# Issuing the context loads of a gated cross-attention kernel from ScalarE's queue instead of SyncE's

## The chip, the cores and the metric

The kernel runs on one core of a Trainium2 chip. A core has five engines with a queue of instructions each: TensorE (PE, matmuls), VectorE (DVE), ScalarE (ACT), GpSimd (POOL) and SyncE (SP). SyncE does no arithmetic; it waits for semaphores and issues transfers (DMAs). ScalarE and GpSimd can issue transfers too. The metric is the device time of one execution in microseconds.

## The reference

The kernel computes one gated cross-attention block and one gated feed-forward block for 32 batches. The queries come from `x` (32 x 100 x 256), keys and values from a context `ctx` (32 x 1444 x 256); there are 16 heads of 16.

```python
h = layernorm(x)
q, k, v = h @ Wq.T + bq, ctx @ Wk.T + bk, ctx @ Wv.T + bv
p = softmax(where(mask, clip(q @ k.T / 4, -50, 50), -50))       # per head
delta = clip(residual_scale, 0, 0.3) * ((p @ v) @ Wo.T + bo)
x = x + tanh(g_xattn) * (norm(delta) * ln_gamma + ln_beta)
x = x + tanh(g_ffn) * ffn(layernorm(x))     # quantized, silu(a) * b, hidden 704
```

## The kernel before, in words

**Tiles and steps.** The 1444 context rows of a batch are cut into NT = 12 tiles of 121 rows (the last has 113), and the tiles into three pieces of four, u = 0, 1, 2. A batch is 12 steps on every engine, n = 0 to 11, one for each tile of scores. Each engine has its own hand-written program; semaphores order them.

**The way of a piece.** `load_c(b, u)` copies a piece of the transposed context from HBM into one of two buffers `c_in` (128 partitions, 2 x 484 floats each). VectorE splits it into a high and a low part, `c_hi` (line 763) and `c_lo` (line 769); the latter raises `split_done` under the names `lo0`, `lo1`, `lo2`. After `c_lo` the buffer `c_in` is free. TensorE computes keys and values from the parts (lines 1293 and 1307), ScalarE and VectorE write the keys' parts `k_hi` and `k_lo`, ScalarE the values `v_sb`. `stack_k(b, u)` on SyncE then copies the keys with 12 transfers of about 121 KB from buffer to buffer into `k_st`, in the layout that the score matmuls read (line 331). `k_st` has two slots for three pieces, so `stack_k` first waits until the scores that read the slot are done (line 328). The scores of steps 0, 4 and 8 wait for the landing of the stack of piece 0, 1 and 2. POOL issues 12 smaller transfers that stack the next batch's queries (`q_st`, line 492) at its step 8.

**When.** Context work runs ahead. In batch b, TensorE computes from step 4 on the keys and values of pieces 0 and 1 of batch b + 1, and in steps 0 to 3 those of piece 2 of b itself. So the stack of piece 0 of batch b + 1 starts after the scores of step 7 of batch b (they free its slot), and must have landed by step 0 of batch b + 1.

**A step.** On TensorE: four score matmuls, half a context item, some other work, sometimes the attention matmuls (`pv`, line 1272, 128 at once in steps 1, 5 and 9), four score matmuls again, the other half of the item. On ScalarE: an item of the context work (`k_hi` or `v_sb`), an exponential of the first scores (line 572), other work, an exponential of the second scores. There are two score banks in turn, so each score matmul waits for the exponential before the last. The feed-forward work is done for groups of 128 rows; 25 such groups end in the 32 batches, so 7 batches (0, 4, 9, 13, 18, 22 and 27) complete none. The batches behind these, and batch 0, have shorter steps in their second half.

**The order of SyncE's queue in a batch** is: stack of piece 1; x of batch b + 2; residual rows; wait for `lo0` of b + 1; load of piece 2 of b + 1; store of a finished group; stack of piece 2; wait for `lo1`; load of piece 0 of b + 2; stack of piece 0 of b + 1; wait for `lo2`; load of piece 1 of b + 2.

The first pieces, before the loop over batches, are loaded from SyncE too. The line numbers are those of the kernel before.

Of the kernel before, what the change touches and what calls it, by code (L numbers as in the profile page):

```python
# [37 lines left out]
def whole(n, base=0):  # L38
    return Batch(base + n, (base + n) // 2, n % 2, base)


def flamingo_block(nc, x, ctxT, maskT, g_xattn, g_ffn, wqT, bq, wkT, bk, wvT, bv, woT, bo,
# [22 lines left out]
    NB, S, H = x.shape  # L65
    T = ctxT.shape[2]
    F = w1T.shape[1]
    P = 128
# [13 lines left out]
    CW = TPC * TT  # L82
    CL = [sum(TL[TPC * u:TPC * (u + 1)]) for u in range(NCH)]
# [24 lines left out]
    with es:  # L108
        def sb(name, shape, dt=f32):
            return es.enter_context(nc.sbuf_tensor(name, shape, dt))  # L110
# [4 lines left out]
        def sem(name):  # L115
            return es.enter_context(nc.semaphore(name))
# [39 lines left out]
        c_in = [sb(f"c_in{i}", [P, KT, CW]) for i in range(2)]  # L156
# [48 lines left out]
        c_loaded = [sem(f"c_loaded{i}") for i in range(2)]  # L205
# [11 lines left out]
        split_done, k_lo_done = sem("split_done"), sem("k_lo_done")  # L217
# [6 lines left out]
        SPLIT = Steps(*(f"{p}{u}" for u in range(NCH) for p in ("hi", "lo")))  # L224
# [31 lines left out]
        def c_slot(b, u):  # L256
            g = b.plus(u)
            before = 3 * b.pair + (3 * b.par + u) // 2
            return g.par, before


        def e_slot(b, n):
            return (NT * b.par + n) % NE

        def full_group(b):

            g = S * (b.row + 1) // P - 1
            if b.row < 0 or g < S * b.row // P:
                return None
            return whole(g, NG if b.base else 0)  # L270
# [38 lines left out]
        def _(sp):  # L309
            def load_x(b):  # L310
                sp.dma_start(x_in[b.par][:, :], x[bass.ds(b.row, 1), :, :].rearrange("o s h -> (o s) h")
                             ).then_inc(x_loaded[b.par], 16)

            def load_c(b, u):
                slot, _n = c_slot(b, u)
                src = ctxT[bass.ds(b.row, 1), :, u * CW:u * CW + CL[u]]
                sp.dma_start(c_in[slot][:, :, 0:CL[u]], src.rearrange("o (k p) t -> p (o k) t", p=P)
                             ).then_inc(c_loaded[slot], 16)

            def stack_k(b, u):  # L320
                slot, _n = c_slot(b, u)
                sp.wait_ge(k_lo_done, KE.after(b, f"{u}{KT - 1}"))
                if not (isinstance(b.n, int) and b.n == 0 and u < NKS):

                    ob, ou = (b, u - NKS) if u >= NKS else (b.plus(-1), u - NKS + NCH)
                    if b.base:
                        sp.sem_inc(waited_sp, 1)
                    sp.wait_ge(sc_ready, SCORE.after(ob, STEPS * TPC * (ou + 1) - 1))
                for j in range(NQ):
                    for part, src in enumerate((k_hi, k_hi, k_lo)):  # L330
                        sp.dma_start(k_st[st_slot(b, u)][QR * part:QR * (part + 1), :, j, 0:CL[u]].bitcast(f32),  # L331
                                     src[slot][QR * j:QR * (j + 1), :, 0:CL[u]].bitcast(f32)
                                     ).then_inc(k_stacked[u], 16)

            def store(g):
                sp.wait_ge(result_done, g.n + 1)
                sp.dma_start(out_rows[P * g.row:P * (g.row + 1), :], y_out[:, :]).then_inc(stored, 16)

            def load_res(g):
                if g.row >= 2:  # L340
                    sp.wait_ge(dve_post, D_V.after(g.plus(-2), "x1"))
                elif g.base:
                    sp.wait_ge(dve_post, D_V.after(whole(NG - 1), "x1"))
                sp.dma_start(x_res[g.par][:, :], x_rows[P * g.row:P * (g.row + 1), :]).then_inc(res_loaded[g.par], 16)
# [21 lines left out]
            def batch(b, own, nxt, nxt2):  # L366
                if own:
                    stack_k(b, 1)
                if nxt2:
                    sp.wait_ge(dve_x, X_V.after(b, "xn"))  # L370
                    load_x(b.plus(2))
                if full_group(b):
                    load_res(full_group(b))
                if nxt:
                    sp.wait_ge(split_done, SPLIT.after(b.plus(1), "lo0"))
                    load_c(b.plus(1), 2)
                if full_group(b.plus(-2)):
                    store(full_group(b.plus(-2)))
                stack_k(b, 2)
                if nxt2:  # L380
                    sp.wait_ge(split_done, SPLIT.after(b.plus(1), "lo1"))
                    load_c(b.plus(2), 0)
                if nxt:
                    stack_k(b.plus(1), 0)
                if nxt2:
                    sp.wait_ge(split_done, SPLIT.after(b.plus(1), "lo2"))
                    load_c(b.plus(2), 1)

            def passes(base):
                if base:  # L390
# [149 lines left out]
        def _(act):  # L540
# [21 lines left out]
            def magnitudes(i):  # L562

                act.wait_ge(s_w, 16 * 6)
                nc.scalar.activation(unused[i], weights[i], ACT.Abs, accum_out=wabs[:, i:i + 1]).then_inc(s_seta, 1)

            def exps(b, n, k):
                q = n * STEPS + k
                act.wait_ge(sc_ready, SCORE.after(b, q))
                if k == 0 and not (isinstance(b.n, int) and b.n == 0 and n < NE):  # L570
                    act.wait_ge(pv_done, TILE.after(b, n) - NE)
                nc.scalar.activation(e_sb[e_slot(b, n)][0:TL[n], k * SW:(k + 1) * SW].rearrange("p (o c) -> p o c", o=2),  # L572
                                     sc[q % NSC][0:TL[n], :, 0:2 * PW],
                                     ACT.Exp, scale=HD ** -0.5).then_inc(exp_done, 1)
# [28 lines left out]
            def ctx_item(b, w):  # L603
                u, r = divmod(w, 4)
                if r < 2:
                    k_head(b, u, r)
                else:
                    v_out(b, u, r - 2)
# [21 lines left out]
            def h_turned(b):  # L630
                act.wait_ge(pe_post, D_T.after(b, "hT"))
                nc.scalar.activation(hT[:, :, :], mb16[:, 0:FT * P].rearrange("p (k s) -> p k s", k=FT), ACT.Copy
                                     ).then_inc(act_post, 1)
# [10 lines left out]
                act.wait_ge(pe_post, D_T.after(b, f"u{i}"))  # L644
                nc.scalar.activation(us[:, cols], mb[:, 0:FH], ACT.Copy, scale=tiny[:, 5:6]).then_inc(act_post, 1)

            def batch(b, own, nxt):
                c, gd, ge = b.plus(1), full_group(b.plus(-1)), full_group(b.plus(-2))
                for n in range(NT):
                    if n < ITEM + 1 and own:  # L650
                        ctx_item(b, n - (ITEM + 1) + NT)
                    if n >= ITEM + 1 and nxt:
                        ctx_item(c, n - (ITEM + 1))
                    exps(b, n, 0)
                    if ge and n == 1:
                        h_turned(ge)
                    if nxt and n == 4:
                        x_turned(c)
                    if nxt and n == 5:
                        x_query(c)  # L660
                    if gd and n == 7:
                        x2_turned(gd)
                    if gd and n in (9, 10):
                        ffn_up(gd, n - 9)
                    if gd and n in (8, 9):
                        ffn_gate(gd, n - 8)
                    exps(b, n, 1)

            def passes(base):
                act.wait_ge(s_setv, SETV["bqm11"])  # L670
                x_turned(whole(0, base))
                x_query(whole(0, base))
                for w in range(NT - (ITEM + 1)):
                    ctx_item(whole(0, base), w)
                    if w >= 3 and not base:
                        for i in range(2 * w - 6, min(2 * w - 4, 6)):
                            magnitudes(i)
                act.wait_ge(s_setv, SETV["bv"])
                act.wait_ge(s_setp, SETP["rest"])
                act.wait_ge(s_seta, SETA["abs5"])  # L680
                for n in range(NB - 1):
                    batch(whole(n, base), True, True)
                e = whole(NB - 1, base)
                batch(e, True, False)
                last = full_group(e)
                h_turned(last.plus(-1))
                x2_turned(last)
                for i in range(2):
                    ffn_gate(last, i, sc[0][:, i, :])
                    ffn_up(last, i, sc[1][:, i, :])  # L690
                h_turned(last)

            passes(0)
            again(act, passes)

# [823 lines left out]
```

## Time and profile before

| | |
|---|---|
| median of 3 runs | 1332.48 us (1331.07 to 1334.24) |
| the profiled execution | 1329.38 us, span 1327.6 us |
| TensorE busy | 1282.6 us |
| VectorE busy | 1069.2 us |
| ScalarE busy | 947.9 us |
| GpSimd busy | 394.4 us |
| granted TensorE clock, mean | 0.987 |

The span is the time from the first to the last instruction that the profiler saw; what lies around it makes the rest of the execution's time. Busy times of the engines overlap each other. The matmuls are pipelined and their ends are modelled, so TensorE can show as busy while it stalls briefly. Issuing a transfer does not count as busy time of an engine; such instructions are listed under the engine's name with a q (SPq, ACTq).

### The profile page before, as it was taken

What the parts mean: (1) busy time and instruction counts of PE and PEld (TensorE: products, weight loads), DVE (VectorE), ACT (ScalarE), POOL (GpSimd) and SP (SyncE); (2) the same over time, 40 slices, a digit from 0 to 9 for tenths busy, and PEclk for the clock granted to TensorE, in tenths of its full rate; (3) what the DMA queues carried; (4) which work ended last, traced back from release to release, by engine and by line L of the source; (5) the groups of instructions that cost most, each with busy time, mean ns of one, the idle gap of its engine ahead of it and who ended that gap; (6) DMA issues with size and microseconds to landing.
All of it is one profiled execution on the core that took longest, in us unless ns stands there. A gap on an engine that the chain in (4) does not pass through costs nothing.

```text
span 1327.6 us, 47302 instructions
## 1 busy us (share of the span) xinstructions
PE 1282.6 (97%) x19802; PEld 1177.7 (89%) x19802; DVE 1069.2 (81%) x2085; ACT 947.9 (71%) x1561; POOL 394.4 (30%) x695
## 2 busy tenths in 40 slices
PE   5999999999999999999999999999999999999983
PEld 4988998999999999999999999999999999999972
DVE  5777888779888789886888886888778889778864
ACT  4766777677777767776767776777777877777761
POOL 4322333222333231322331323331233331133310
PEclk9999999999999999999999999999999999999986
DMA  8867777677777777777676768766777776777630
GB/s 238 204 161 180 168 171 183 168 173 182 170 170 184 174 175 174 169 170 197 171 171 168 178 160 203 174 168 160 175 188 176 180 170 163 179 182 175 149 78 11
DMA packets 146187, 225.38 MB, mean 170 GB/s; under 512 B 29674, under 2 KB 139310, under 8 KB 145966
## 3 DMA queue, kind: packets, MB, share of 16 engines
q1 hardware_dynamic: 132312, 202.06, 62.5%
q0 software_dynamic: 12288, 19.69, 6.4%
q8 instruction: 158, 2.59, 0.9%
q10 hardware_dynamic: 1366, 0.53, 0.2%
q14 instruction: 63, 0.52, 0.1%
HBM read 57.27 MB, written 3.28 MB: 46 GB/s over the span
## 4 chain that ended last, share of the span: by engine, by line
PE 89%; SPq 4%; DVE 3%; DMA 2%; issue 1%; ACT 1%; POOL 0%; DVEq 0%; POOLq 0%; ACTq 0%
PE sc L1252 23%; PE pvb L1272 20%; PE cb L1307 19%; PE cb L1293 18%; SPq L331 4%; PE mb L1367 2%; PE mb L1335 2%; PE mb L1345 2%; DMA k_st<-k_lo 1%; PE mb L1382 1%; DVE zt L880 1%; PE mb L1374 1%; PE mb L1328 0%; DMA c_in<-in_ctxT 0%; DVE k_lo L793 0%
## 5 line engine op out<-in xcount | busy, mean ns | idle before, releaser
L572 ACT ACTIVATE e_sb<-sc 121x800 f32<-121x800 f32 (+1 forms) x768 | 644.7, 844 | 187.2 <-PE sc L1252 176.5
L1252 PE MATMUL sc<-q_st,k_st 96*121 96x200 f32 (+1 forms) x3072 | 469.4, 275 | 8.3 <-DMA k_st<-k_lo 5.2
L1252 PEld LDWEIGHTS sc<-q_st,k_st 96*121 96x121 f32 (+1 forms) x3072 | 411.1, 185 | 40.0 <-issue 9.0
L802 DVE TENSOR_SCALAR e_sb<-e_sb,hi_b 121x1600 f32<-121x1600 f32 (+1 forms) x384 | 404.2, 1056 | 12.3 <-ACT e_sb L572 12.1
L1272 PE MATMUL pvb<-e_sb,v_sb 121*32 121x100 f32 x12288 | 286.5, 251 | 0.0
L1272 PEld LDWEIGHTS pvb<-e_sb,v_sb 121*32 121x32 f32 x12288 | 265.2, 110 | 23.5 <-issue 20.4
L793 DVE SCALAR_TENSOR_TENSOR k_lo<-cb,bk_c,k_hi 128x484 fp32r<-128x484 f32 (+1 forms) x192 | 134.5, 701 | 132.8 <-ACT k_hi L584 132.5
L492 POOL DMA_DIRECT2D q_st<-bd_hi x256 | 157.5, 619 | 269.2 <-DVE bd_lo L848 263.8
L1307 PE MATMUL cb<-wv_hi,c_hi 128*121 128x256 f32 (+1 forms) x768 | 221.7, 289 | 2.4 <-DVE k_lo L793 1.3
L1307 PE MATMUL cb<-wv_hi,c_lo 128*121 128x256 f32 (+1 forms) x768 | 215.6, 281 | 0.0
L1307 PE MATMUL cb<-wv_lo,c_hi 128*121 128x256 f32 (+1 forms) x768 | 215.5, 281 | 0.0
L1293 PE MATMUL cb<-c_hi,wk_hi 128*128 128x484 f32 (+1 forms) x384 | 153.7, 400 | 0.0
L1293 PE MATMUL cb<-c_hi,wk_lo 128*128 128x484 f32 (+1 forms) x384 | 146.3, 381 | 0.0
L1293 PE MATMUL cb<-c_lo,wk_hi 128*128 128x484 f32 (+1 forms) x384 | 146.2, 381 | 0.0
L1307 PEld LDWEIGHTS cb<-wv_hi,c_hi 128*121 128x121 f32 (+1 forms) x768 | 141.2, 184 | 4.4 <-DVE k_lo L793 4.4
L1307 PEld LDWEIGHTS cb<-wv_hi,c_lo 128*121 128x121 f32 (+1 forms) x768 | 140.3, 183 | 0.0
L1307 PEld LDWEIGHTS cb<-wv_lo,c_hi 128*121 128x121 f32 (+1 forms) x768 | 139.6, 182 | 0.0
L584 ACT ACTIVATE k_hi<-cb,bk_c 128x484 fp32r<-128x484 f32 (+1 forms) x192 | 127.0, 661 | 1.3 <-PE cb L1293 1.3
L769 DVE TENSOR_TENSOR c_lo<-c_in,c_hi 128x968 fp32r<-128x968 f32 (+1 forms) x96 | 118.7, 1237 | 0.0
L463 POOL TENSOR_SCALAR d_ve<-dmv,scal 128x1 f32<-128x1 f32 x25 | 10.9, 438 | 344.2 <-DVE dmv L907 344.2
L593 ACT ACTIVATE v_sb<-cb 121x512 f32<-121x512 f32 x160 | 96.1, 600 | 5.3 <-PE cb L1307 5.3
L492 POOL DMA_DIRECT2D q_st<-bd_lo x128 | 88.2, 689 | 0.1
(160 smaller groups left out, 1351.1 us busy)
## 6 DMA issues: line engine op xcount, KB each, us to landing
k_st<-k_hi SPq DMA_DIRECT2D x512, 121.0 KB, 3.0
c_in<-in_ctxT SPq DMA_DIRECT2D x64, 484.0 KB, 3.9
k_st<-k_lo SPq DMA_DIRECT2D x256, 121.0 KB, 3.2
k_st<-k_hi SPq DMA_DIRECT2D x256, 119.0 KB, 3.3
c_in<-in_ctxT SPq DMA_DIRECT2D x32, 476.0 KB, 3.8
k_st<-k_lo SPq DMA_DIRECT2D x128, 119.0 KB, 3.0
q_st<-bd_hi POOLq DMA_DIRECT2D x256, 50.0 KB, 3.3
q_st<-bd_lo POOLq DMA_DIRECT2D x128, 50.0 KB, 3.2
```

Of the source, the lines that this page charges most:

```text
L331: sp.dma_start(k_st[st_slot(b, u)][QR * part:QR * (part + 1), :, j, 0:CL[u]].bitcast(f32), src[slot][QR * j:QR * (j + 1), :, 0:CL[u]].bitc ...
L492: nc.gpsimd.dma_start(q_st[b.par][QR * part:QR * (part + 1), :, j, :].bitcast(f32), src[QR * j:QR * (j + 1), :, :, :].rearrange("p k a s - ...
L572: nc.scalar.activation(e_sb[e_slot(b, n)][0:TL[n], k * SW:(k + 1) * SW].rearrange("p (o c) -> p o c", o=2), sc[q % NSC][0:TL[n], :, 0:2 * PW],
L584: nc.scalar.activation(k_hi[slot][:, o, 0:CL[u]], cb[o][:, 0:CL[u]], ACT.Identity, bias=bk_c[:, o:o + 1]).then_inc(k_hi_done, 1)
L593: nc.scalar.activation(v_sb[0:TL[n], n:n + 2, :, 0:4:3, :].rearrange("p n q a d -> p (n q) a d"), cb[i][0:TL[n], :].rearrange("p (q a d) - ...
L769: V.tensor_tensor(c_lo[slot][:, :, 0:w], c_in[slot][:, :, 0:w], c_hi[slot][:, :, 0:w].bitcast(f32), ALU.subtract).then_inc(split_done, 1)
L793: V.scalar_tensor_tensor(k_lo[slot][:, o, 0:w], cb[o][:, 0:w], bk_c[:, o:o + 1], k_hi[slot][:, o, 0:w].bitcast(f32), ALU.add, ALU.subtract ...
L802: V.tensor_scalar(e, e, E_LO, hi_b[b.par][0:TL[n], n:n + 1], ALU.max, ALU.min).then_inc(clip_done, 1)
L1252: last = T_.matmul(sc[q % NSC][0:TL[n], e // 2, (e % 2) * PW:(e % 2 + 1) * PW], k_st[st_slot(b, n // TPC)][:, pr // NQ, pr % NQ, t0:t0 + T ...
L1272: last = T_.matmul(pvb[QR * j:QR * (j + 1), col:col + S], v_sb[0:TL[n], n, pr, 2 * a:2 * a + 2, :].rearrange("p x d -> p (x d)"), e[0:TL[n ...
L1293: last = T_.matmul(cb[o][:, 0:w], wt[:, k, o * P:(o + 1) * P], ct[slot][:, k, 0:w], start=i == 0, stop=i == 5)
L1307: last = T_.matmul(cb[i][0:TL[n], half * H:(half + 1) * H], ct[slot][:, k, t0:t0 + TL[n]], wt[:, k, :], start=(k == 0 and a == 0), stop=(k ...
```

## The change

The three loads of a batch and the waits ahead of them leave SyncE's queue. ScalarE gets a `load_c` of its own and issues the same three transfers, behind the same waits, at the end of step 4 (piece 2 of batch b + 1), step 7 (piece 0 of b + 2) and step 11 (piece 1 of b + 2), each behind the second exponential of that step. The loads before the loop over batches stay on SyncE.

```diff
             def batch(b, own, nxt, nxt2):
...
-                if nxt:
-                    sp.wait_ge(split_done, SPLIT.after(b.plus(1), "lo0"))
-                    load_c(b.plus(1), 2)
                 if full_group(b.plus(-2)):
                     store(full_group(b.plus(-2)))
                 stack_k(b, 2)
-                if nxt2:
-                    sp.wait_ge(split_done, SPLIT.after(b.plus(1), "lo1"))
-                    load_c(b.plus(2), 0)
                 if nxt:
                     stack_k(b.plus(1), 0)
-                if nxt2:
-                    sp.wait_ge(split_done, SPLIT.after(b.plus(1), "lo2"))
-                    load_c(b.plus(2), 1)
...
+            def load_c(b, u):
+                slot, _n = c_slot(b, u)
+                src = ctxT[bass.ds(b.row, 1), :, u * CW:u * CW + CL[u]]
+                act.dma_start(c_in[slot][:, :, 0:CL[u]], src.rearrange("o (k p) t -> p (o k) t", p=P)
+                              ).then_inc(c_loaded[slot], 16)
...
                     exps(b, n, 1)
+                    if nxt and n == 4:
+                        act.wait_ge(split_done, SPLIT.after(c, "lo0"))
+                        load_c(c, 2)
+                    if nxt and nxt2 and n == 7:
+                        act.wait_ge(split_done, SPLIT.after(c, "lo1"))
+                        load_c(b.plus(2), 0)
+                    if nxt and nxt2 and n == 11:
+                        act.wait_ge(split_done, SPLIT.after(c, "lo2"))
+                        load_c(b.plus(2), 1)
```

## Rows read from the trace of the kernel before

**Rows 1.** The page: busy time, share of the span, instructions

```profile
PE 1282.6 (97%) x19802; PEld 1177.7 (89%) x19802; DVE 1069.2 (81%) x2085; ACT 947.9 (71%) x1561; POOL 394.4 (30%) x695
```

**Rows 2.** Waits, all engines: us in total, times, longest

```profile
PEld sc L1252 <- DMA k_st<-k_lo: 7.3, 10, 1.6
```

**Rows 3.** Waits of SyncE's queue: us in total, times, longest

```profile
SPq L317 <- DVE c_lo L769: 110.2, 30, 6.1
```

**Rows 4.** Timeline of SyncE in batch 9: start, duration (us), what

```profile
408.93 0.59 SPq L317 DMA_DIRECT2D c_in<-in_ctxT  x1
412.72 1.23 SPq L331 DMA_DIRECT2D k_st<-k_hi  x2
...
421.34 1.61 SPq L331 DMA_DIRECT2D k_st<-k_lo  x1
423.00 0.59 SPq L317 DMA_DIRECT2D c_in<-in_ctxT  x1
```

**Rows 5.** Timeline of TensorE, score matmuls of batches 9 to 11

```profile
411.98 0.65 PE L1252 MATMUL sc<-q_st,k_st 96*121 96x200 f32 x4
...
415.69 0.58 PE L1252 MATMUL sc<-q_st,k_st 96*121 96x200 f32 x4
...
426.32 0.58 PE L1252 MATMUL sc<-q_st,k_st 96*121 96x200 f32 x4
...
428.48 0.57 PE L1252 MATMUL sc<-q_st,k_st 96*121 96x200 f32 x4
...
464.23 0.67 PE L1252 MATMUL sc<-q_st,k_st 96*121 96x200 f32 x4
```

**Rows 6.** Transfers into k_st, window 422 to 423 (the issue from 421.34)

```profile
DMA to landing us min/median/max: 3.8/3.8/3.8
```

**Rows 7.** Timeline of SyncE in batch 10, first and last issue of the stack

```profile
451.80 1.22 SPq L331 DMA_DIRECT2D k_st<-k_hi  x2
...
461.83 0.60 SPq L331 DMA_DIRECT2D k_st<-k_lo  x1
```

**Rows 8.** Transfers into k_st, window 462 to 463 (the issue from 461.83)

```profile
DMA to landing us min/median/max: 2.4/2.4/2.4
```

**Rows 9.** Timeline of SyncE: first issue of the first and last of 31 stacks

```profile
54.76 1.23 SPq L331 DMA_DIRECT2D k_st<-k_hi  x2
...
1243.27 1.23 SPq L331 DMA_DIRECT2D k_st<-k_hi  x2
```

**Rows 10.** Stretch 413 to 426: busy by engine, granted clock, DMA share, GB/s

```profile
413.00:426.00 13.00, 13.00 (x205) 11.58 (x205) 9.23 (x18) 10.49 (x19) 7.79 (x14) 1.00 0.83 197
```

**Rows 11.** Timeline of SyncE: first issue, first and last of 28 piece-1 stacks

```profile
146.52 0.59 SPq L331 DMA_DIRECT2D k_st<-k_hi  x1
...
1216.16 1.23 SPq L331 DMA_DIRECT2D k_st<-k_hi  x2
```

**Rows 12.** Issues of line 317: duration ns minimum/median/maximum, first and last start

```profile
L317 SPq DMA_DIRECT2D c_in<-in_ctxT x96: 372/586/1616, 1.7 to 1229.8; - x96
```

**Rows 13.** Timeline of VectorE in batch 9, c_lo of piece 1

```profile
406.89 1.16 DVE L769 TENSOR_TENSOR c_lo<-c_in,c_hi 128x968 fp32r<-128x968 f32 x1
```

**Rows 14.** Timeline of ScalarE: exponentials of steps 7, 8 and the next 0

```profile
412.66 0.84 ACT L572 ACTIVATE e_sb<-sc 121x800 f32<-121x800 f32 x1
...
413.88 0.83 ACT L572 ACTIVATE e_sb<-sc 121x800 f32<-121x800 f32 x1
...
427.02 0.84 ACT L572 ACTIVATE e_sb<-sc 121x800 f32<-121x800 f32 x1
```

**Rows 15.** Timeline of ScalarE's queue at the start

```profile
1.70 0.51 ACTq L544 DMA_DIRECT2D bk_c<-in_bk  x1
```

**Rows 16.** The page, DMA issues: count, KB each, median us to landing

```profile
c_in<-in_ctxT SPq DMA_DIRECT2D x64, 484.0 KB, 3.9
```

**Rows 17.** The page, DMA queues: packets, MB, share of 16 engines' span

```profile
q1 hardware_dynamic: 132312, 202.06, 62.5%
q0 software_dynamic: 12288, 19.69, 6.4%
```

More of the change, by code:

```diff
@@ L645, in ffn_up, with batch @@
                 nc.scalar.activation(us[:, cols], mb[:, 0:FH], ACT.Copy, scale=tiny[:, 5:6]).then_inc(act_post, 1)
-            def batch(b, own, nxt):
+            def batch(b, own, nxt, nxt2=False):
                 c, gd, ge = b.plus(1), full_group(b.plus(-1)), full_group(b.plus(-2))
@@ L680, in passes @@
                 act.wait_ge(s_seta, SETA["abs5"])
-                for n in range(NB - 1):
-                    batch(whole(n, base), True, True)
+                for n in range(NB - 2):
+                    batch(whole(n, base), True, True, True)
+                batch(whole(NB - 2, base), True, True)
                 e = whole(NB - 1, base)
```

## The prediction, made before the changed kernel was timed

> **What bounds the kernel now.** I read the page's busy shares first. TensorE is busy 1282.6 us, 97% of the span [rows 1]. So a transfer can cost or give time only where it makes TensorE wait, and the first question is for which transfers it waits. In the view of waits the largest one in the steady part is the stacked keys', 7.3 us in 10 pieces on the weight load's side [rows 2]. No wait for a context piece stands there. On SyncE's queue 110.2 us go to the waits for c_lo ahead of a load, which the change takes off that queue [rows 3]. That is idle time of a queue, and it matters only if what is queued behind comes late.
>
> Next I put the three stacks of a batch beside their deadlines. Piece 0 of the next batch is the tight one. In batch 9 its first issue starts at 412.72 us [rows 4], freed by the second scores of step 7 (411.98, 0.65 long) [rows 5]. Its last issue starts at 421.34 and lands 3.8 us later, at 425.2 [rows 4, 6]. TensorE wants it at 426.32 [rows 5]: latency 12.5 us, room 13.6 us. Batch 10 has no row group to finish, so its steps are shorter: start 451.80, last issue 461.83, landing 2.4 us on, at 464.2, where the scores start at once, at 464.23 [rows 5, 7, 8]. There the room is 12.4 us and nothing is spare. I took the latency of all 31 such stacks (the first issued at 54.76, the last at 1243.27 [rows 9]): 11.5 to 14.7 us, mean 12.8; 12.4 in the 8 short batches, 13.0 in the 23 long ones.
>
> Why is this stack slow? Its 12 issues go out two in 1.23 us when nothing holds them, so all in some 7.7 us; here they take 10.2, the last alone 1.61 [rows 4]. POOL issues the query stack in the same stretch (its step 8), and the DMA share there is 0.83 [rows 10]. The stack of piece 1, without POOL's transfers beside it, has a mean latency of 11.1 us over the 28 of batches 3 to 30 (the first from 146.52, the last from 1216.16 [rows 11]).
>
> **The change, part by part.**
>
> *SyncE loses three issues and three waits.* One issue is 0.37 to 1.62 us, median 0.59 [rows 12]. Piece 2's load stands just ahead of the stack of piece 2. That stack can start up to one issue earlier, but TensorE is not seen waiting for it in the steady part: worth nothing. Piece 1's load (423.00) follows the tight stack, and the next stack must wait for the last scores of the batch anyway: nothing in issue time. The tight stack itself waits for scores 7 and not for the load ahead of it, issued 3.8 us before [rows 4]: nothing.
>
> *ScalarE gains three waits and three issues.* The waits are met: c_lo of piece 1 ends at 408.05 [rows 13], and step 7 ends on ScalarE at 413.50 [rows 14]; the other two stand likewise. The bounds of an issue are 0.37 and 1.62 us, SyncE's fastest and slowest of the same transfer [rows 12]. I take 0.6: its median, and close to the 0.51 that an issue on ScalarE takes at the start, at 1.70, beside the first of SyncE's loads at 1.7 [rows 12, 15]. Queued behind step 7's issue are a copy to v_sb and the exponential that ends at 413.88 + 0.83 = 414.71 [rows 14]; TensorE's scores of step 9 need its bank at 415.69 [rows 5]: cover 1.0 us. Behind step 11's are a copy and the exponential that ends at 427.86 [rows 14], which the scores of step 1 need at 428.48 [rows 5]: cover 0.6 us. Behind step 4's come the attention matmuls of step 5, when ScalarE idles. So the issues cost 0 at my value. At 1.62 us the two exposed places cost 0.6 + 1.0 us a batch, 48 us over 30 batches, the far bound.
> The Trainium skill (Perfetto Trace Analysis, "DMA Instruction — HWDGE (DVE, Sync)") says that a sequencer must lock the descriptor generator for itself and that the profiled duration holds the wait for that lock. By it a ScalarE issue could take its own time plus one of SyncE's, an estimate of 1.2 us, and cost 0.6 us a batch at the tighter place; the two side by side at the start do not bear that out.
>
> *The loads move in time and to another queue.* This decides. Piece 2's goes from just ahead of its batch's stack of piece 2 into that stack. Piece 1's goes from 423.00 to just before the exponential at 427.02 [rows 4, 14], into the stack of the next piece 1, which has the room: four steps. Piece 0's was issued at 408.93 and landed about 3.9 us later [rows 4, 16], just when the tight stack starts. It goes to 413.5, 0.8 us *after* that start, into the stretch where POOL's transfers run too.
>
> What do a load's 484 KB [rows 16] cost there? Queue 1 spends 62.5% of 16 engines' span on 202.06 MB, 4.1 us per MB, so a load (0.496 MB) is 2.0 us of all engines. The query stack is 6.4% of the span over 32 batches, 2.7 us each [rows 17]. Lower bound of the delay: 0 (a gain is the second rival). The share of 0.83 over 13 us leaves 2.2 us idle, which could hold all of it; and the mean latency of 11.1 us of piece 1 is had with a load ahead of it in the same queue. Upper bound: all 2.0 us plus one issue of 0.6, so 2.6 us. Nearest row: POOL's 2.7 us. The stack takes 11.1 us without it and 12.8 with it: 1.7 of 2.7, two thirds. Two thirds of 2.0 is 1.3; I take off 0.3, because piece 1's load no longer follows the stack's last pieces closely. Delay 1.0 us.
> The Trainium skill (DMA: Bandwidth & Descriptors, "Queues, rings and completion order") has each DMA engine serve its queues in turn, packet by packet. Where SyncE's queue kept the load ahead of the stack or behind it, a second queue mixes it in; that speaks for a full delay while all three queues have work. With 2.0 us the same sum below would give 42 us.
>
> **Sum.** The delay counts only beyond the room. The 8 short batches have none, so each pays nearly all: 6.6 us (batch 0 has 0.9 us spare). Of the 22 long ones with a moved load, six have latencies of 13.5 or more and pay nearly all, 5.9 us; the other 16 have 0.6 to 1.4 us spare and pay 1.6 between them. Together 14.1 us. On the profiled execution's 1329.4 us (span 1327.6 and 1.8 around it) that is 1343.5. The median of the runs is 3.1 us above that execution, so 1346.6: I say 1347. The same adding for other delays: 0.5 gives 6 us, 1.5 gives 28, 2.6 gives 60.
>
> **Rivals.**
> - *The load is absorbed.* For it: idle DMA time of 2.2 us in the stretch, and piece 1's example. By the skill's section "Issuing engines are not separate DMA queues" (same page) the same 16 engines carry the same bytes and only issue time is saved. Time: delay under 0.25 us, 0 to 2.5 us, 1332 to 1335.
> - *Faster: SyncE's lighter queue ends the waits for stacked keys.* The tight stack's last pieces would no longer share the engines with piece 1's load, issued 0.05 us after them. If that shortens the landing by more than the moved load costs (those of two last pieces took 3.8 and 2.4 us [rows 6, 8]), the steady waits vanish; those are 3.5 us by my sum, and at most the 7.3 us of rows 2. Time: 1326 to 1329. Against it: the load is back after the stack's landing, and one as large is put into its middle.
> - *ScalarE pays.* Its issues take over 1.2 us because SyncE's issues are stuck behind full queues. It decides from 0.6 us on at step 0. Time: +10 to +48 us, 1342 to 1380.
>
> **How the numbers follow.** Stacked keys late: 0.60. Absorbed: 0.20. Faster: 0.14. ScalarE pays: 0.06. Least that can be told from no change is 0.2%, 2.7 us. Some of the first case's small delays fall within it, some of the absorbed one's outside: faster 0.14, same 0.21, slower 0.65. The likeliest case alone spans 1337 to 1375 (delay 0.5 to 2.0). For 8 in 10, I go from 1331 (nearly all of the faster case left out) to 1369 (delay up to 1.8).
>
> **What would show it.** In the changed kernel: piece 0's load on ScalarE's queue starts 0.7 to 1.0 us after the stack's first issue; more of that stack's issues take over 1 us; its latency goes from 12.8 to near 13.8; the waits for k_st by TensorE rise from 7 to about 20 us, nearly all at step 0 of a batch, most in the short ones. The durations of ScalarE's issues stay below 1 us, and waits for e_sb do not grow. I am wrong if the latency stays at 12.8 (absorbed) or falls (faster), or if the new idle time of TensorE is before scores and released by ScalarE.

## The result, and the profile after

The changed kernel takes 1350.89 us, the median of 4 runs (1348.23 to 1356.21). The kernel before, run beside it, takes 1333.35 us (4 runs, 1331.07 to 1334.24). The ratio is 1.0138 [1.0115, 1.0162]: slower by 17.5 us. The prediction was 1347.0, range 1331 to 1369. The profiled execution took 1348.23 us, with a span of 1346.3 us (before: 1327.6). The mean granted clock is 0.986, as good as the 0.987 of before, so the time is not a matter of the clock.

The page of the changed kernel: busy times, then two queues of part 3 (packets, MB, share of 16 engines' span), then the shares of the chain that ended last, then the transfers (KB each, median us from issue to landing).

```profile
PE 1290.9 (96%) x19802; PEld 1182.0 (88%) x19802; DVE 1069.6 (79%) x2085; ACT 950.2 (71%) x1561; POOL 392.2 (29%) x695
...
q1 hardware_dynamic: 107560, 157.21, 49.7%
q10 hardware_dynamic: 26118, 45.38, 13.5%
...
PE 75%; SPq 12%; DMA 6%; DVE 3%; issue 2%; ACT 1%; POOL 0%; DVEq 0%; POOLq 0%
...
c_in<-in_ctxT ACTq DMA_DIRECT2D x60, 484.0 KB, 4.6
```

No engine has more work than in [rows 1], to within 1%. Queue 1 (SyncE's) carries 44.85 MB less than in [rows 17], and queue 10 (ScalarE's), which had 0.53 MB before, carries just that much more. The bytes did not change, only their queue and their moment. The chain now runs for 12% through SyncE's issues and for 6% through transfers, where before it had 4% and 2%:

```profile
PE 89%; SPq 4%; DVE 3%; DMA 2%; issue 1%; ACT 1%; POOL 0%; DVEq 0%; POOLq 0%; ACTq 0%
```

The waits of the changed kernel (total us, times, longest):

```profile
PEld pvb L1279 <- issue: 25.0, 68, 1.6
PEld sc L1259 <- DMA k_st<-k_lo: 16.4, 21, 2.0
PE sc L1259 <- DMA k_st<-k_lo: 11.8, 16, 1.8
PE pvb L1279 <- issue: 3.6, 5, 1.4
...
PE sc L1259 <- ACT e_sb L569: 1.9, 4, 0.6
```

The wait for stacked keys grew by 9.1 us from the 7.3 of [rows 2]. A second wait grew too, "issue" at the attention matmuls, where nothing that the profile shows is waited for. Here is the same view of the kernel before:

```profile
PEld pvb L1272 <- issue: 20.4, 64, 0.6
```

Its total rose by 4.6 us: 3.1 us of that stand at step 1, in several batches, and 1.6 us at step 9, where one batch (28) has the longest, 1.6.

Now the tight stack that is issued in batch 9, which [rows 4] show before. SyncE's timeline in the changed kernel (start, duration, what):

```profile
419.04 1.23 SPq L331 DMA_DIRECT2D k_st<-k_hi  x2
...
422.23 1.37 SPq L331 DMA_DIRECT2D k_st<-k_lo  x1
423.64 2.06 SPq L331 DMA_DIRECT2D k_st<-k_hi  x2
...
427.83 0.96 SPq L331 DMA_DIRECT2D k_st<-k_lo  x1
432.18 1.23 SPq L331 DMA_DIRECT2D k_st<-k_hi  x2
```

ScalarE's timeline in the same moment:

```profile
419.00 0.84 ACT L569 ACTIVATE e_sb<-sc 121x800 f32<-121x800 f32 x1
419.00 0.37 ACTq L561 DMA_DIRECT2D c_in<-in_ctxT  x1
419.74 0.59 ACT L590 ACTIVATE v_sb<-cb 121x512 f32<-121x512 f32 x1
```

The load is issued at 419.00, 0.04 us before the stack's first issue. It takes 0.37 us, while ScalarE's exponential runs, and the copy behind is not held up. These are the landings of the stack's transfers issued from 419.04 and, below, of those issued from 427.83:

```profile
DMA to landing us min/median/max: 5.1/5.1/5.1
...
DMA to landing us min/median/max: 5.3/5.3/5.3
```

Before, the last one took 3.8 us [rows 6], and the first, in the view of transfers from 412.8 to 413:

```profile
DMA to landing us min/median/max: 2.4/2.4/2.4
```

So the stack of batch 9 lands at 427.83 + 5.3 = 433.1, 14.1 us after its start (12.5 before), and TensorE waits for it at step 0 (timeline of TensorE, changed kernel; in brackets the idle time before):

```profile
431.54 0.56 PE L1259 MATMUL sc<-q_st,k_st 96*113 96x200 f32 x4
...
433.19 0.67 PE L1259 MATMUL sc<-q_st,k_st 96*121 96x200 f32 x4 [0.37 <-DMA k_st<-k_lo]
```

**Where the 18.7 us of span went.** I read the start of each group of score matmuls in both traces and added up, over the batches, by how much each interval between two neighbouring groups grew.

| place | growth, us |
|---|---|
| last scores of step 11 to first scores of step 0 | 8.0 |
| step 0 itself | 1.2 |
| step 1, and the interval behind it | 4.6 + 0.8 |
| from the second scores of step 10 to the first of step 11 | 0.4 |
| step 9 itself (1.7 in batch 28, 0.8 in batch 31) | 2.5 |
| until the first scores of batch 1 | 1.6 |
| sum | 19.1 |

What lies behind the last scores is 0.4 us shorter. The stall for keys explains half (9.2 us, which fits the 9.1 in the waits). As the prediction said, most of it falls on the short batches: 5.7 of the 8.0 us. The 4.6 at step 1 equals the 4.6 by which "issue" rose only by chance, since 1.6 of the latter stand at step 9. The idle time before a matmul shows less than the delay, because the ends of matmuls are modelled. These growths are differences of two single executions. How much two profiles of one kernel differ is told at the end of the experiments.

### The profile page after: what moved, and what is told of

It reads as the page before. It is cut to its first block, busy times and chain, and to the rows that moved or that the text cites. A ratio compares the mean times of both kernels' runs of the same rounds, so it can differ in the third digit from the quotient of the medians.

```text
span 1346.3 us, 47302 instructions
## 1 busy us (share of the span) xinstructions
PE 1290.9 (96%) x19802; PEld 1182.0 (88%) x19802; DVE 1069.6 (79%) x2085; ACT 950.2 (71%) x1561; POOL 392.2 (29%) x695
## 4 chain that ended last, share of the span: by engine, by line
PE 75%; SPq 12%; DMA 6%; DVE 3%; issue 2%; ACT 1%; POOL 0%; DVEq 0%; POOLq 0%
PE sc L1259 19%; PE pvb L1279 17%; PE cb L1300 15%; PE cb L1314 15%; SPq L331 12%; DMA k_st<-k_lo 5%; PE mb L1342 2%; PE mb L1352 2%; PE mb L1374 2%; PE mb L1389 1%; PE mb L1381 1%; DVE zt L887 1%; DMA c_in<-in_ctxT 0%; PE mb L1335 0%; DVE k_lo L800 0%
## 5 line engine op out<-in xcount | busy, mean ns | idle before, releaser
L1259 PEld LDWEIGHTS sc<-q_st,k_st 96*121 96x121 f32 (+1 forms) x3072 | 410.8, 185 | 48.7 <-DMA k_st<-k_lo 16.4
L809 DVE TENSOR_SCALAR e_sb<-e_sb,hi_b 121x1600 f32<-121x1600 f32 (+1 forms) x384 | 405.5, 1058 | 14.6 <-ACT e_sb L569 14.3
L483 POOL DMA_DIRECT2D q_st<-bd_lo x128 | 85.0, 664 | 0.1
```

The lines of the kernel that those rows point to most:

```text
L483: nc.gpsimd.dma_start(q_st[b.par][QR * part:QR * (part + 1), :, j, :].bitcast(f32), src[QR * j:QR * (j + 1), :, :, :].rearrange("p k a s - ...
L809: V.tensor_scalar(e, e, E_LO, hi_b[b.par][0:TL[n], n:n + 1], ALU.max, ALU.min).then_inc(clip_done, 1)
L1259: last = T_.matmul(sc[q % NSC][0:TL[n], e // 2, (e % 2) * PW:(e % 2 + 1) * PW], k_st[st_slot(b, n // TPC)][:, pr // NQ, pr % NQ, t0:t0 + T ...
```

## The experiments

Each kernel's time is a median, with the ratio to the kernel before, which was timed beside it. Its median was 1332.31 beside e1 to e4, 1332.35 beside e5 to e8 and 1331.94 beside e9 and e10. "Latency" is from the first issue of a stack of piece 0 to its last landing, a mean over 31 stacks; it is 12.83 before and 13.67 in the changed kernel.

### One load at a time

Three kernels start from the one before and move a single load, the others staying on SyncE.

```diff
-                if nxt2:                     # e1; e2 and e3 alike with lo0 / lo2
-                    sp.wait_ge(split_done, SPLIT.after(b.plus(1), "lo1"))
-                    load_c(b.plus(2), 0)
...
+                    if nxt and nxt2 and n == 7:        # e2: n == 4, e3: n == 11
+                        act.wait_ge(split_done, SPLIT.after(c, "lo1"))
+                        load_c(b.plus(2), 0)
```

> Only the load of piece 0 moves to ScalarE (end of step 7); the loads of pieces 2 and 1 stay on SyncE where they were. Theory A (the moved load delays the tight stack of piece 0): that stack's mean latency rises from 12.8 to 13.5 or more, TensorE's added time before step 0 is most of the 8.0 us that the full change showed there, and the time is 7 to 14 us above before. Rival B (most of the loss comes from the other two loads, through ScalarE or through something of TensorE's own at step 1): 0 to 4 us above before.

> Only the load of piece 2 moves to ScalarE (end of step 4). Theory A and its rivals agree: this stack has about 2 us to spare, so 0 to 2 us above before. More than 3 us would show that one of the 30 issues on ScalarE costs by itself, whichever place it has.

> Only the load of piece 1 moves to ScalarE (end of step 11). Theory A alone: the next stack has the room, and the tight stack no longer has this load behind it, so -3 to +1 us against before. Theory C (this load runs where TensorE fetches the code of its attention matmuls of step 1, and delays that): 3 to 7 us above before, with step 1 longer by about 1 us in some six batches and idle time marked as issue ahead of the attention matmuls.

| kernel | median, us | ratio | latency |
|---|---|---|---|
| e1, piece 0 (step 7) | 1374.11 (1365.02 to 1380.8) | 1.0296 [1.0258, 1.0334] | 14.34 |
| e2, piece 2 (step 4) | 1331.78 | 0.9989 [0.9970, 1.0009] | 12.72 |
| e3, piece 1 (step 11) | 1333.26 | 0.9998 [0.9981, 1.0015] | 12.66 |

Piece 0's load alone costs 41.8 us, far above the 7 to 14 that I had expected and more than the whole change. The waits of e1:

```profile
PEld sc L1259 <- DMA k_st<-k_lo: 35.1, 30, 2.7
PE sc L1259 <- DMA k_st<-k_lo: 28.8, 29, 2.5
```

Nearly every batch now waits. The stack's first eleven transfers land nearly as in the changed kernel (the last of them 12.8 us after the start, against 12.7); the twelfth lands at 14.3, against 13.7. The difference in the program there is piece 1's load, which in e1 is still the next thing in SyncE's queue (piece 2's differs too, and e2 gives nothing for it). So that load costs the last transfer some 0.7 us when piece 0's load runs beside the stack, and moving it away pays part of piece 0's bill. When piece 0's load is not there (e3) the same move gives 0.2 us.

The intervals from the last scores of step 11 to the first of step 0 grew by 29.8 us in e1 (batch 1's included), near the 28 that the prediction's table has for a delay of 1.5 us. Another 10.7 us came within step 0, 9.3 of them in six batches: a longer wait brings another loss with it. These are windows of e1's batch 1 (columns: length; busy PE, PEld, DVE, ACT, POOL; granted clock; DMA share; GB/s):

```profile
70.00:73.00 3.00, 0.00 (x0) 0.00 (x0) 1.54 (x3) 0.00 (x0) 0.49 (x1) 1.00 1.07 251
73.00:77.00 4.00, 3.75 (x14) 3.45 (x15) 0.00 (x0) 1.68 (x2) 0.00 (x0) 0.57 1.02 227
```

TensorE has nothing to do for the 3 us up to 73; just after, the granted clock is 0.57 in the mean over four microseconds, for 3.4 us of which it is at the lower level of 1.2 GHz. Six such stretches of 3.4 us stand in e1's steady part, in the same six batches; none stands in that of the changed kernel.

e2 says that piece 2's move is worth nothing, as said in the prediction. e3 is a sum of two things, though its time is that of the kernel before. Step 1 gets longer by 3.8 + 1.0 us, and as the median did not rise, about as much must be gained elsewhere. Ahead of step 0 its profile is 1.8 us shorter over batches 1 to 31, but a second profile of the unchanged kernel is so too (1.7 us, see the end of this section), so the profile does not show where the gain is. The wait "issue" is there too:

```profile
PE pvb L1279 <- issue: 1.4, 3, 0.7
```

### The moment or the queue

e4 starts from the kernel before. All loads stay on SyncE; only the moment of piece 0's moves, to where the change has it, by a wait for the scores of step 7 (the same that the tight stack waits for).

```diff
                 if nxt2:
                     sp.wait_ge(split_done, SPLIT.after(b.plus(1), "lo1"))
+                    sp.wait_ge(sc_ready, SCORE.after(b, STEPS * TPC * 2 - 1))
                     load_c(b.plus(2), 0)
```

> The kernel before with one edit: SyncE issues the load of piece 0 only when the scores of step 7 are done, directly ahead of the tight stack. The moment is that of the full change, the queue is the old one. Theory A in the form that the moment decides: 7 to 14 us above before, latency of the tight stack (from its own first issue) 13 us or more. Rival in the form that the second queue decides (packets of two queues mixed): the delay is smaller than with piece 0 alone on ScalarE by half or more, 0 to 5 us above before.

It took 1354.33 us (1347.29 to 1365.56), ratio 1.0157 [1.0120, 1.0194], above the 7 to 14 us expected; latency 13.61 from the stack's own first issue (the profile is of its slowest execution). No load left SyncE's queue, and the loss is there. The moment is enough for it. Against e1, which differs in the queue of this load alone, the loss is half (22.0 of 41.8 us), so a second queue makes it worse. A half of a loss that grows steeply with the delay is a small part of the delay: 13.61 and 0.5 for the load's issue, which starts the stack later, against 14.34.

### Moving the loads within the change

```diff
-                    if nxt and nxt2 and n == 7:
+                    if nxt and nxt2 and n == 5:        # e5: piece 0
...
-                    if nxt and nxt2 and n == 11:
-                        act.wait_ge(split_done, SPLIT.after(c, "lo2"))
-                        load_c(b.plus(2), 1)
+                    if nxt and b.row > 0 and n == 1:   # e6: piece 1, in the next batch
+                        act.wait_ge(split_done, SPLIT.after(b, "lo2"))
+                        load_c(c, 1)
```

e7 has both edits.

> The full change, but the load of piece 0 stands at the end of step 5 on ScalarE's queue (after the same wait) and not at the end of step 7, so that it lands before the tight stack starts. Theory A (its moment in the stretch of the tight stack is the loss): latency of the tight stack back at 12.6, nothing added before step 0, and the time from +18 us down to -2 to +4 us against before; what is left above 0 is the step 1 loss of piece 1's load (4.7 us in the profile of piece 1 alone). Rival B (ScalarE's issues as such cost): still 8 us or more above before.

> The full change, but the load of piece 1 is issued at the end of step 1 of the next batch, not at the end of step 11. Theory C (issued at step 11 it delays the fetch of TensorE's code for the attention matmuls of step 1): the lengthening of step 1 in some six batches, about 5 us, is gone, and the tight stack stays free of a load behind it, so 11 to 15 us above before. If the step 1 loss is of another cause, 17 to 20 us above before, with step 1 as long as in the full change.

> Both moves: piece 0 at the end of step 5, piece 1 at the end of step 1 of the next batch, piece 2 at the end of step 4. Theories A and C together: no load within the stretch of the tight stack, none ahead of step 1, and the last transfer of the tight stack alone in its queue: 1 to 5 us below before. If one of them is wrong, 2 us or more above before.

| kernel | median, us | ratio | latency | ahead of step 0, us | step 1, us |
|---|---|---|---|---|---|
| changed | 1350.89 | 1.0138 [1.0115, 1.0162] | 13.67 | +8.0 | +4.6, +0.8 |
| e5 | 1332.91 | 1.0000 [0.9987, 1.0013] | 12.66 | -1.6 | +2.8, +1.4 |
| e6 | 1345.45 | 1.0098 [1.0076, 1.0121] | 13.63 | +9.1 | 0.0 |
| e7 | 1331.89 | 0.9987 [0.9975, 0.9999] | 12.65 | -2.7 | 0.0 |

The last two columns are growths against the kernel before, worked out as in the table of the result. e5 wins the whole loss of keys back and leaves the one at step 1; e6 the other way round. So the two losses have different causes, one for each load. In e6's waits both are to be read:

```profile
PEld pvb L1279 <- issue: 21.0, 65, 0.6
PEld sc L1259 <- DMA k_st<-k_lo: 17.3, 21, 2.0
```

e7, without either loss, was expected 1 to 5 us below the kernel before. Its interval reaches from 0.1 to 3.3 us below, its median is 0.5 below. It has a loss of its own: the load at step 1 falls into the stack of piece 1, whose mean latency is 13.2 us (11.1 before), and 1.7 us are added ahead of step 4.

What the loss at step 1 is, the traffic of batch 7 shows. In the changed kernel TensorE's attention matmuls of step 1 break off after 126 of 128 (timeline):

```profile
312.20 0.58 PE L1259 MATMUL sc<-q_st,k_st 96*121 96x200 f32 x4
...
313.37 2.96 PE L1279 MATMUL pvb<-e_sb,v_sb 121*32 121x100 f32 x126
...
317.01 0.33 PE L1279 MATMUL pvb<-e_sb,v_sb 113*32 113x100 f32 x2 [0.68 <-issue]
...
317.59 0.65 PE L1259 MATMUL sc<-q_st,k_st 96*121 96x200 f32 x4
```

In e6 they run through:

```profile
308.68 0.58 PE L1259 MATMUL sc<-q_st,k_st 96*121 96x200 f32 x4
309.85 2.97 PE L1279 MATMUL pvb<-e_sb,v_sb 121*32 121x100 f32 x128
...
313.08 0.65 PE L1259 MATMUL sc<-q_st,k_st 96*121 96x200 f32 x4
```

From score group to score group that is 5.39 against 4.40 us. The queues of the changed kernel from 312 to 314 (packets, MB, share of the 16 engines in the window), and then from 314 to 315:

```profile
q1 hardware_dynamic: 183, 0.30, 65.0%
q10 hardware_dynamic: 170, 0.30, 40.3%
...
q1 hardware_dynamic: 152, 0.24, 100.6%
q8 instruction: 1, 0.02, 7.8%
```

and of e6 from 309 to 310:

```profile
q1 hardware_dynamic: 124, 0.18, 79.3%
q8 instruction: 1, 0.02, 6.4%
```

Queue 8 moves the program's own instructions. In batch 7 of e6 such a packet goes 0.5 us after the first scores of step 1; in the changed kernel it goes 2.0 us after them, 1.1 us after piece 1's load (queue 10) has left the engines, while queue 1 fills them. It is alike in batches 6, 7, 15, 16, 24 and 25, which make the 4.6 us: 1.4 to 2.2 us behind the scores in the changed kernel, 1.2 at the latest in e6, and TensorE 0.4 to 1.0 us late. Within one batch the delay follows the packet from kernel to kernel. For batch 24:

| kernel | packet behind the first scores of step 1, us | to the second scores, us |
|---|---|---|
| before | -0.9 | 4.06 |
| e5 | 0.0 | 4.07 |
| e3 | 1.2 | 4.68 |
| changed | 1.7 | 4.96 |
| e8 (below) | 2.0 | 5.26 |

Not every late packet stops TensorE: in batch 8 of the changed kernel one goes at 2.4 us and nothing is late. That TensorE stopped for the instructions of that very packet is the reading that fits; no row names it.

The 1.7 us at step 9 of batch 28 have the same marks, but they come with piece 0's load. In the changed kernel:

```profile
1183.73 0.57 PE L1259 MATMUL sc<-q_st,k_st 96*121 96x200 f32 x4
1184.92 2.94 PE L1279 MATMUL pvb<-e_sb,v_sb 121*32 121x100 f32 x122
1189.23 0.37 PE L1279 MATMUL pvb<-e_sb,v_sb 121*32 121x100 f32 x6 [1.38 <-issue]
```

A packet of queue 8 goes 2.7 us behind the first of these rows. In all kernels with piece 0's load at the tight stack (changed, e1, e4, e6, e9) it goes 1.8 to 3.7 us behind it, and that interval is 0.7 to 2.7 us longer. In all others, e8 with half of the load among them, it goes at 1.3 at the latest and the interval is as before. In e4 the load is on SyncE's queue, so this too is a matter of the moment.

### Half of the load

e8 is the changed kernel with a smaller piece 0. It leaves out the second half of the columns of piece 0 for all loads on ScalarE's queue, so part of the context is not transferred.

```diff
-                act.dma_start(c_in[slot][:, :, 0:CL[u]], src.rearrange("o (k p) t -> p (o k) t", p=P)
+                w = CL[u] if u else CL[u] // 2
+                act.dma_start(c_in[slot][:, :, 0:w], src[:, :, 0:w].rearrange("o (k p) t -> p (o k) t", p=P)
```

> The full change, but each load of piece 0 on ScalarE's queue moves only the first half of its columns (242 of 484 KB); the other half keeps old data, so this leaves out a part of the transfers. Theory A in the form that the delay follows the bytes of the load: latency of the tight stack 13.2 instead of 13.7, time 7 to 12 us above before. Rival: the delay comes from there being a transfer of a second queue at all (a fixed cost): latency 13.5 or more, 15 us or more above before.

It took 1336.73 us, ratio 1.0025 [1.0012, 1.0039], 4.4 us above the kernel before, where I had expected 7 to 12. The latency is 13.06, between the 12.66 of e5 (nothing in the stretch) and the 13.67 of the changed kernel (all of it). Half of the bytes make 0.4 of the 1.0 us. The number of pieces is the same and only their size is halved, so the delay follows the bytes, and not the instruction or the pieces.

### A start behind the stack's first issue

In the prediction the load came 0.8 us behind the stack's start. e9 makes that so.

```diff
                     if nxt and nxt2 and n == 7:
                         act.wait_ge(split_done, SPLIT.after(c, "lo1"))
+                        act.wait_ge(exp_done, SCORE.after(b, 7 * STEPS + 1))
                         load_c(b.plus(2), 0)
```

> The full change with one wait more: ScalarE's load of piece 0 also waits until the second exponential of step 7 is done. In the full change it started about 0.03 us before the first issue of the tight stack; here it should start some 0.8 us after, as the prediction had it. If a transfer that starts ahead takes the engines whole and the order matters (theory D), the stack's first transfer lands at 2.5 us again instead of 5.1, but the load's bytes still stand between the later ones, so the last one lands as late: latency 13.4 to 13.8, time 12 to 20 us above before. If the late start lets the load use idle engine time only (rival), latency under 13.2 and under 8 us above before.

The load is issued 0.87 us behind the first issue of the stack. The first transfer then lands after 2.6 us again and not after 5.1, but the whole stack still takes 13.68 us. The time is 1351.63 (1347.4 to 1360.88), ratio 1.0154 [1.0124, 1.0184], the same as the changed kernel's. Which transfers of the stack are late does not matter; when the last one lands does.

### The part that may pay

From e3 and e6: piece 1's load off the tail of the tight stack, and off step 1. e10 is e3 with the load at the end of step 2 of the next batch; the other two loads stay on SyncE.

```diff
-                    if nxt and nxt2 and n == 11:
-                        act.wait_ge(split_done, SPLIT.after(c, "lo2"))
-                        load_c(b.plus(2), 1)
+                    if nxt and b.row > 0 and n == 2:
+                        act.wait_ge(split_done, SPLIT.after(b, "lo2"))
+                        load_c(c, 1)
```

> The kernel before with piece 1's load alone on ScalarE, at the end of step 2 of the next batch; the loads of pieces 2 and 0 stay on SyncE. By theories A and C this takes the load from behind the tight stack (gain of about 2 us before step 0) without the step 1 loss and without putting it into the middle of the stack of piece 1: 2 to 4 us below before, ratio 0.997 to 0.9985. If it is not below before, the gain before step 0 is given back by the stack of piece 1 (waits before step 4).

It took 1329.23 us (1326.31 to 1332.95), ratio 0.9971 [0.9956, 0.9985]. That is 2.7 us below the kernel before, and the best of all; against e3 it is 4.0 us lower, which fits e3's 4.7 us at step 1. The gain is small, at the bound of what can be told, and its profile (span 1331.1) is of its slowest execution, in which one late stack in batch 1 costs some 5 us with 6.8 us at the lower clock behind it. So the profile does not show the gain of the median, and that the gain lies ahead of step 0 is argued, not shown.

### The kernel before, profiled again

> The kernel before, unchanged, profiled once more as a control. The first scores came at 31.7 us in its first profile and at 33.4 to 34.5 us in all the changed ones. If that difference is of the execution and not of the edits, they come after 33 us here as well, with the clock granted at half for 3.4 us shortly after 20 us.

1329.87 us, span 1328.1. All edited kernels had their first scores at 33.4 to 34.5 us; this had them at 32.5 (31.7 in the first profile), and my expectation of 33 or more missed. The other half of it missed too: every edited kernel has 3.4 us at the lower clock shortly after 20 us, and the unchanged one has none in either profile. Why is open. But the first scores of batch 1 stand at 70.1 us here, at 68.4 in the other profile of the same kernel, and at 70.0 in the changed one. So the 1.6 us "until the first scores of batch 1" is within the scatter of one kernel.

This profile also bounds what the tables of growths can tell. Ahead of step 0 it is 1.7 us shorter than the first one, over batches 1 to 31. So the -1.6 of e5, the -1.8 of e3 and the -1.7 of e10 show no gain, and the -2.7 of e7 hardly one (with the interval ahead of batch 1 counted in, all four are 2.1 to 3.2 us below this profile); the +8.0 of the changed kernel would be +9.7 against this profile. At step 1 and at step 9 of batch 28 the two agree within 0.1 us. Its waits give the scatter of the others:

```profile
PEld pvb L1272 <- issue: 20.2, 63, 0.6
PEld sc L1252 <- DMA k_st<-k_lo: 6.1, 8, 2.0
```

The 7.3 of [rows 2] stands against 6.1; the latency is 12.81 against 12.83.

## Why the prediction came out right, point by point

**What bounds, and which deadline is tight.** Right. TensorE stalls where the tight stack is late, at step 0, and the loss goes (e5) when the load leaves that stretch. It comes with that load alone (e1), and on SyncE's queue too (e4).

**The delay of 1.0 us.** Measured: 0.84 against the kernel before. Its two terms were both too small, with opposite signs. For the load beside the stack I took 1.3; e1 shows 14.34 - 12.83 = 1.5, inside my bounds of 0 and 2.6. For piece 1's load gone from the tail I took off 0.3; e1 against the changed kernel makes it 0.67 (and e3, without piece 0's load beside the stack, 0.17). 1.5 - 0.67 is the 0.84.

**More issues of the stack over 1 us**, one of my signs: not borne out. Of the 372 issues of these stacks 95 take over 1 us (94 before). From the start of the first issue to the end of the last a tight stack takes 10.54 us in the mean (10.32 before); from there to its landing it takes 3.12 (2.51 before). Most of the delay of 0.84 us is behind the last issue, so SyncE's durations hardly show it.

**The time of the load's start.** Wrong, without effect: 0.8 us behind the stack's first issue in the prediction, 0.04 ahead of it in the trace (419.00 and 419.04 in batch 9). I had let the issue wait for the exponential ahead of it. e9 shows that the stack takes as long either way.

**The sum of 14.1 us.** The median is 3.9 us above my number, but two errors stand against each other in it, so that it came so near is in part luck. Step 0 paid 9.2 us (11.3 against the second profile of before), not 14.1: the delay was 0.84, and my table of delays gives some 11.5 for that. Added again from the trace, batch by batch, the same rule gives 13.8 for a delay of 1.0 and 10.7 for 0.84. The wait for keys came to 16.4 us, where I had said about 20. The rest was not in the sum at all: 5.4 us at step 1, from piece 1's load, and 1.7 us at step 9 of batch 28, from piece 0's. The prediction had looked at the stacks that the loads fall into, and said rightly that piece 1's has room; it had not asked which other traffic goes in those stretches. The step that failed is "into the stack of the next piece 1, which has the room". It had also called the 7.3 us of [rows 2] the largest wait in the steady part; the same view had 20.4 us of "issue" at the attention matmuls, and that row is the one that grew beside it. Of the ends that I gave the likeliest case, the lower one by my own sum is 1338, not 1337.

**ScalarE pays nothing.** Right. The issue takes 0.37 us where I had taken 0.6; TensorE's waits for e_sb are 1.9 us (1.6 before, 1.9 in its second profile). That rival is refuted, with its bound of 48 us. The issues of all loads on ScalarE's queue (ns), and one of them with the SyncE issues around it (the first row is two of 0.6 us each):

```profile
L561 ACTq DMA_DIRECT2D c_in<-in_ctxT x91: 374/374/406, 46.0 to 1250.5; - x91
...
83.82 1.24 SPq L331 DMA_DIRECT2D k_st<-k_hi  x2
...
84.32 0.37 ACTq L561 DMA_DIRECT2D c_in<-in_ctxT  x1
```

By the Trainium skill (Perfetto Trace Analysis, "DMA Instruction — HWDGE (DVE, Sync)") the profiled duration holds the wait for the lock of the descriptor generator, and from that I had an estimate of 1.2 us. This case shows no such wait: 31 of the 91 issues begin while SyncE is in the middle of one, and none takes over 0.41 us.

**The rival that it is absorbed** had the 2.2 us of idle DMA time for it. The time is not free, since the load does not spread over it. This is the changed kernel's traffic from 420 to 422:

```profile
q10 hardware_dynamic: 183, 0.35, 90.0%
```

It is the only queue there. For two microseconds the load had the 16 engines to itself; the stack of queue 1, issued from 419.04 on, moved nothing, and neither did POOL's transfers. Before, in the same stretch of the stack (413.5 to 415.5), the engines looked like this:

```profile
q1 hardware_dynamic: 139, 0.24, 57.2%
q0 software_dynamic: 32, 0.05, 13.2%
```

Idle share is there, 30%. But of the load's 2.0 us of work 1.5 stayed as a delay in e1, so the stack catches up only in part. The Trainium skill (DMA: Bandwidth & Descriptors, "Queues, rings and completion order") says that a DMA engine "drains a whole packet (≈9-17 descriptors typical, spec ceiling ≤64) from one row's ring before switching". I had read that as mixing. A load of 128 x 2 rows of 484 floats is 256 pieces of 1936 bytes, so 16 for each of the 16 engines: all of it can be one such packet, and the row above agrees with that. The trace does not say which packets the engines take as a whole, so this is a reading.

**The faster rival** had a true mechanism and the wrong sign in sum. Taking piece 1's load from the tail gives 0.67 us in e1 against the changed kernel and 0.17 us in e3, and e10, which moves that load alone (to step 2 of the next batch), is 0.29% faster, at the bound of what can be told. It needs piece 0's load out of the tight stack's stretch.

## What to carry to other kernels

Place a bulk load by the deadline of what else is under way when it goes, not by which queue has time: the same load costs nothing that can be told at step 5 (e5) and 18.0 us more at step 7 (1350.89 against 1332.91). For each moment that a load is moved to, go through all queues of that stretch, the one that moves the program's instructions too. And keep the queue empty of other work just behind the last transfer of a stack that is waited for; here that was worth 0.2 to 0.7 us a stack. Profile the unchanged kernel twice before reading gains of 1 or 2 us out of a difference of two traces.

## What the runs showed of the hardware

- A load of 484 KB on a second queue did not mix with the first queue's transfers in small parts. It had 90.0% of the 16 engines for 2 us, and no other queue had any. In e9, where the load comes 0.87 us later, its queue had the engines in the same way (from 422 to 423):

```profile
q10 hardware_dynamic: 180, 0.34, 92.4%
q0 software_dynamic: 6, 0.02, 5.1%
q1 hardware_dynamic: 1, 0.00, 0.5%
```

- ScalarE's queue issued the load at 419.00, at the same time as the exponential ahead of it in the program began (419.00, 0.84 long). The issue behind an operation did not wait for the end of the operation.
- The program's own instructions are fetched by the same DMA engines (queue 8), and where a load of 484 KB goes in the same stretch, such a packet is seen later (in batch 7 at 2.0 us behind the first scores of step 1, without the load at 0.5), with TensorE 0.4 to 1.0 us late in six batches. That it stopped for that packet is inferred.
- In e1 TensorE had no matmul for 1.6 to 4.2 us, six times, and each time 3.4 us at the lower level of the granted clock, 1.2 GHz, followed (0.57 in the mean of the window from 73 to 77 us). A gap was not always followed by it: one of 2.2 us in the second profile of the kernel before (at 67.9) was not, and none of the changed kernel's, up to 1.5 us, in its steady part.
